# A fused tokenizer, phase-memory attention and top-2 mixture of experts on one core: less side work, a hand-written order, and two PSUM banks for the later pairs

## The chip, the cores and the metric

One core of a Trainium2 chip runs the whole kernel in one launch. The metric is the device time in microseconds (us) of one execution, as the median of several. The host only lays data out.

## The reference, cut to what matters

Sixteen images and sixteen texts become sixteen sequences of 272 tokens of 64 features; everything is fp32.

```python
h = tokenizer(x)                      # 2x2 conv, q, k, v, softmax over 144 tokens, output projection
h = concatenate([h, txt], axis=1)     # (16, 144 + 128, 64)
h = h + attention(layernorm(h))
h = h + experts(layernorm(h))

# attention: a content stream, a position stream, a mix of both
kp = tanh(tanh(x @ Wk1 + bk1) @ Wk2 + bk2) * pi      # 32 phases a token; qp the same with Wq
mem_re, mem_im = cumsum(cos(kp) * v_c), cumsum(sin(kp) * v_c)        # along the tokens
content = (mem_re * cos(qp) + mem_im * sin(qp)).sum() / sqrt(32 * pos)
position = (cumsum(v_p * cos_p) * cos_p + cumsum(v_p * sin_p) * sin_p) / sqrt(pos)
gate = softmax(relu(x @ Wg1 + bg1) @ Wg2 + bg2)
out = layernorm(gate[0] * position + gate[1] * content) @ Wo + bo    # with ln_g, ln_b

# experts: 8 of them, top 2 of a gate, computed for all tokens and weighted
for e in range(8):
    out += w[:, e] * (gelu(x @ W1[e] + b1[e]) @ W2[e] + b2[e])
```

## The kernel before, in words

Two sequences lie on the 128 partitions at once (64 features each), so there are 8 pairs of 272 columns, 2176 columns in all. For everything that works on tokens they are cut in 17 windows of 128 columns, in 5 groups of 3, 4, 4, 4 and 2 windows (`GW`). The stages are:

- Pairs, stage by stage: `qkv`, `scores`, `exps`, `probs_n`, `probs_t`, `mix`, `tok_out` (the tokenizer), then `hidden` and `phases` (tanh), `phase_abs`, `trig` (Sin), `content` and `content_b` (the content value and its bias), `values` and `streams` (the position value, and its cumulative sums), `memory` (key times query, masked: the cumulative sum written as a matrix) and `recall` (that matrix times the content value).
- Groups: `h0_t`, `ln1_stats`, `ln1_norm`, `xn_t`, `residual`, `mix_gate`, `gate_z`, `gate_t`, `gate_p` before the attention; `combine`, `ln2_stats`, `ln2_norm`, `norm_s`, `attn_out`, `ln3_stats`, `ln3_norm`, `xn2_t`, `route`, `route_t`, `weights_t`, `route_bias` behind it.
- Steps of the experts: `expert:i` (L1025; first product on TensorE, Gelu on ScalarE, L535) and `expert_out:i` (L1044; second product, times the routing weight on VectorE, L779, added up on GpSimd, L410), with i = 8 g + e for group g and expert e; `finish` transposes a group's sum and adds the residual.

One list, `PLAN` (L131), gives the order of all stages. Each engine walks through it and issues its own part, so every queue has this order and a waiting instruction holds up all behind it. `make_plan` (L114) makes the list from tables of slots and orders: a pair's or a group's stage stands at a fixed offset from the others. All of `recall:0` to `recall:7` stands ahead of `expert:1`. `WARM` puts `keep_warm` steps in the list: 22 matmuls on ones into bank 7 (L815) that compute nothing. SyncE has an order of its own (L336): routing rows out to DRAM and spread over the partitions into `wide` for group g + 1, then the store of group g.

PSUM has 8 banks. `hidden` writes 2 and 3, `phases` 4 and 5, `values` 0, `content` 1, `memory` 2 and 3 or 4 and 5 in turn, `recall` 1; `expert` 0 to 3, `expert_out` 4 or 5; the groups' stages use 6 and 7, for which `take` (L796) keeps the last reader and waits for it. So the first `expert` waits until all values, memories and recalls are read (L1028).

The layer norms are `moments` (L583: statistics block by block, then small operations) and `normalise` (L600): one VectorE operation for each block of 64 columns. Between them GpSimd takes the power -0.5 (L370). The bias of the experts is a product of its own for each group (`route_bias`: L1016 and a copy on VectorE, L771) with which the sum begins.

In `recall` the half h is the outer loop and the three chunks of tokens the inner one (L965); in `memory` the half is the inner one (L953). `phases` contracts over 128 rows of `attw`, half of which are zero (L937).

ScalarE functions by table: exps, then all tanh, then all Sin (`trig`, L502 and L504), then Gelu with the tanh of `route_t`.

Of the kernel before, what the change touches and what calls it, by code (L numbers as in the profile page):

```python
# [21 lines left out]
ACT = mybir.ActivationFunctionType  # L22
# [46 lines left out]
for _name, _n in [("kq1", 128), ("vc", 64), ("vp", 256), ("g1", 16), ("gate", 8)]:  # L69
# [8 lines left out]
PAIR_AT = {  # L78
    "qkv": (0, 0), "scores": (1, 1), "exps": (1, 4.7), "probs_n": (2, 0.5), "probs_t": (2, 4.5),
    "mix": (3, 3), "tok_out": (4, 4), "hidden": (9, 8), "phases": (10, 7.5), "phase_abs": (11, 0.4),  # L80
    "content": (11, 8.5), "content_b": (12, 0.5), "values": (15, 8.6), "streams": (16, 0.6),
    "memory": (18, 8), "recall": (20, 7.5),
}
LN1_AT = {
    "h0_t": (5, 2.5), "ln1_stats": (6, 0.2), "ln1_norm": (6, 8.7), "xn_t": (7, 2.7),
    "residual": (7, 6.5), "mix_gate": (8, 6.784), "gate_z": (9, 0.2), "gate_t": (9, 7.6),
    "gate_p": (10, 12.2),
}
FIRST_AT = {
    "combine": (-7, 7.682), "ln2_stats": (-7, 8.2), "ln2_norm": (-6, 9), "norm_s": (-4, 0.7),  # L90
    "attn_out": (-4, 8.41), "ln3_stats": (-4, 8.6), "ln3_norm": (-2, 0.7), "xn2_t": (-1, 0.7),
    "route": (-1, 4.204), "route_t": (0, 10.2), "weights_t": (1, 8.5), "route_bias": (1, 10.2),
}
LATER_AT = {
    "combine": (-10, 10.6), "ln2_stats": (-10, 12), "ln2_norm": (-8, 0.05), "norm_s": (-7, 5.5),
    "attn_out": (-7, 10.2), "ln3_stats": (-7, 12), "ln3_norm": (-6, 11.4), "xn2_t": (-4, 10.2),
    "route": (-4, 10.998), "route_t": (-2, 0.3), "weights_t": (-2, 10.1), "route_bias": (0, 10.3),
}
EXPERT_AT = {
    "expert": (0, 10), "expert_out": (1, 10.5),  # L100
}
TRIG_AT = [
    (18, 1), (18, 1.1), (19, 19.372), (19, 20), (20, 20), (21, 20), (22, 20.53), (23, 20),
]
EXPERTS = 28
LN1_SHIFT = [0, 0, 0, 0, 0]
SHIFT = [0, 1, 1, 1, 1]
WARM = [
    (10, 9.5, 2), (12, 9.5, 2), (13, 9.5, 2), (14, 9.5, 2), (15, 9.5, 2), (17, 9.5, 2), (27, 0.5, 4),
    (28, 10.05, 6),  # L110
]


def make_plan():  # L114

    plan = [(slot, order, "keep_warm", n) for slot, order, n in WARM]
    for b in range(NP):
        plan += [(slot + b, order, stage, b) for stage, (slot, order) in PAIR_AT.items()]
    plan += [(slot, order, "trig", b) for b, (slot, order) in enumerate(TRIG_AT)]
    for g in range(NG):  # L120
        plan += [(slot + LAST_PAIR[g] + LN1_SHIFT[g], order, stage, g) for stage, (slot, order) in LN1_AT.items()]
        start = EXPERTS + E * g
        steps = FIRST_AT if g == 0 else LATER_AT
        plan += [(slot + start + SHIFT[g], order, stage, g) for stage, (slot, order) in steps.items()]
        for e in range(E):
            plan += [(slot + start + e, order, stage, E * g + e) for stage, (slot, order) in EXPERT_AT.items()]
        plan.append((start + E + 1, 10.7, "finish", g))
    return [(stage, i) for _, _, stage, i in sorted(plan)]


PLAN = make_plan()  # L131


def fusion_block(nc, x_a, x_b, cols_d, tokw_d, phase_d, rows_d, attw_d, spl_d, txt_d, const_d, w1_d,
                 w2_d, b2_d, sel_d, out):
    with ExitStack() as ctx:
# [66 lines left out]
        vare = sb("vare", [128, 2, 8])  # L203
        rstd = sb("rstd", [128, 2, 8])
# [4 lines left out]
        ones = sb("ones", [128, L])  # L209
        cons = sb("cons", [128, COLS])  # L210
# [7 lines left out]
        c1 = sb("c1", [128, 512])  # L218
# [6 lines left out]
        k1 = sb("k1", [128, 8, 8])  # L225
        k2 = sb("k2", [128, 8, 8])
# [918 lines left out]
```

## Time and profile before

| | us |
|---|---|
| median of three runs | 320.4 |
| lowest and highest of them | 315.83, 320.89 |
| the profiled execution, its own time | 314.21 |
| its span, first to last instruction | 312.3 |
| busy: TensorE, VectorE, ScalarE, GpSimd | 277.1, 201.4, 152.2, 111.9 |
| weight loads, beside the matmuls | 145.7 |
| mean granted TensorE clock | 0.952 |

A row of the profile names a line of the kernel, an engine, what is written from what, how often, the busy time, the mean of one in ns, and the idle time before with what ended it. An fp32 matmul shows as two instructions. PE is TensorE, DVE VectorE, ACT ScalarE, POOL GpSimd, SPq the queue in which SyncE issues transfers.

### The profile page before, as it was taken

How to read it: one execution, taken by the hardware profiler on the slowest of the kernel's cores; microseconds unless marked ns; L12 is line 12 of the kernel's file. 1: busy time of each engine (PE TensorE's matmuls, PEld its weight loads, DVE VectorE, ACT ScalarE, POOL GpSimd, SP SyncE). 2: the span in 40 equal slices, each digit the busy share in tenths (PEclk: the TensorE clock that was granted, in tenths of full speed). 3: DMA queues.
4: the chain of work that ended last, by engine and by line, in shares of the span. 5: the costliest groups of instructions: out<-in, count | busy, mean ns of one | idle time of the engine just before them, and what ended most of it. 6: DMA issues, size and time to landing. Idle time of an engine off the chain costs nothing.

```text
span 312.3 us, 4746 instructions
## 1 busy us (share of the span) xinstructions
PE 277.1 (89%) x1576; PEld 145.7 (47%) x1576; DVE 201.4 (65%) x635; ACT 152.2 (49%) x299; POOL 111.9 (36%) x116
## 2 busy tenths in 40 slices
PE   8659795979788896999999889999899999999993
PEld 6547564556454553666445333333333333333551
DVE  4797877379458999858376674575745865645321
ACT  3768761455427531314545536544356546445461
POOL 1100235237627975310252242531524332432332
PEclk9999955699799998999999999999999999999998
DMA  7700000000000000000340291004710057000600
GB/s 244 258 7 1 2 0 0 0 2 1 0 2 2 2 0 0 3 0 0 79 127 0 66 210 25 2 0 104 168 35 3 0 121 173 14 0 4 168 4 17
DMA packets 12360, 14.42 MB, mean 46 GB/s; under 512 B 6097, under 2 KB 9985, under 8 KB 12209
## 3 DMA queue, kind: packets, MB, share of 16 engines
q1 hardware_dynamic: 11760, 13.66, 16.9%
q10 hardware_dynamic: 576, 0.47, 0.6%
q8 instruction: 13, 0.21, 0.3%
q14 instruction: 11, 0.08, 0.1%
HBM read 12.87 MB, written 1.25 MB: 45 GB/s over the span
## 4 chain that ended last, share of the span: by engine, by line
PE 61%; DVE 25%; issue 8%; POOL 2%; ACT 2%; DMA 1%; POOLq 0%; DVEq 0%
PE ps L1055 18%; PE ps L1041 16%; PE ps L968 4%; PE ps L815 3%; DVE arena L569 2%; PE ps L939 2%; PE ps L848 2%; DVE xn L603 2%; DVE early L685 2%; DVE early L680 2%; PE ps L994 2%; DVE early_p L638 1%; PE ps L884 1%; PE ps L1002 1%; DVE vs L779 1%
## 5 line engine op out<-in xcount | busy, mean ns | idle before, releaser
L535 ACT ACTIVATE arena<-ps,cols 128x1024 f32<-128x1024 f32 (+2 forms) x80 | 74.5, 982 | 61.0 <-PE ps L1041 60.9
L410 POOL TENSOR_TENSOR moe<-moe,vs 128x512 f32<-128x512 f32 (+2 forms) x40 | 44.3, 1107 | 91.2 <-DVE vs L779 91.0
L1041 PE MATMUL ps<-xt,w 64*128 64x512 f32 (+2 forms) x320 | 69.3, 551 | 0.0
L1055 PE MATMUL ps<-arena,w 128*64 128x512 f32 (+2 forms) x320 | 67.2, 541 | 0.0
L779 DVE TENSOR_TENSOR vs<-ps,wide 128x512 f32<-128x512 f32 (+2 forms) x40 | 24.4, 610 | 50.0 <-PE ps L1055 45.1
L370 POOL TENSOR_TENSOR rstd<-vare,minus_half 128x8 f32<-128x8 f32 (+2 forms) x15 | 22.8, 1521 | 65.0 <-DVE vare L597 65.0
L1041 PEld LDWEIGHTS ps<-xt,w 64*128 64x128 f32 x320 | 27.5, 186 | 33.5 <-issue 30.9
L1055 PEld LDWEIGHTS ps<-arena,w 128*64 128x64 f32 x320 | 19.4, 136 | 36.3 <-issue 30.5
L603 DVE TENSOR_SCALAR xn<-res,mean,rstd 128x64 f32<-128x64 f32 x68 | 20.0, 365 | 1.4 <-POOL rstd L370 1.4
L968 PE MATMUL ps<-early_p,vc 128*64 128x272 f32 (+2 forms) x96 | 18.9, 322 | 0.0
L968 PEld LDWEIGHTS ps<-early_p,vc 128*64 128x64 f32 (+1 forms) x96 | 11.0, 141 | 9.1 <-issue 6.1
L685 DVE TENSOR_TENSOR_SCAN early<-ones,early 128x272 f32<-128x272 f32 x16 | 14.4, 941 | 0.3
L603 DVE TENSOR_SCALAR comb<-comb,mean,rstd 128x64 f32<-128x64 f32 x34 | 11.6, 410 | 3.4 <-POOL rstd L370 3.4
L508 ACT ACTIVATE cons<-ps 128x272 f32<-128x272 f32 x8 | 3.2, 398 | 21.8 <-PE ps L968 21.8
L389 POOL TENSOR_TENSOR vc<-vc,rows 128x256 f32<-128x256 f32 x8 | 6.7, 832 | 17.1 <-ACT vc L493 17.1
L815 PE MATMUL ps<-ones 128*128 128x272 f32 x44 | 12.0, 407 | 0.6 <-DVE comb L716 0.6
L446 ACT ACTIVATE early_p<-ps,negmax 72x144 f32<-72x144 f32 x32 | 11.6, 372 | 0.4 <-DVE negmax L631 0.4
L848 PE MATMUL ps<-ident,early_p 72*72 72x72 f32 x64 | 6.5, 254 | 6.0 <-DVE early_p L638 6.0
L486 ACT ACTIVATE trig<-ps,cols 128x272 f32<-128x272 f32 x8 | 3.9, 487 | 16.1 <-PE ps L939 16.1
L691 DVE SCALAR_TENSOR_TENSOR trig<-trig,cols 128x544 f32<-128x544 f32 x8 | 6.3, 784 | 8.4 <-ACT trig L487 8.4
L588 DVE BATCH_NORM_STATS2 stat<-res 128x6 f32<-128x64 f32 x68 | 9.5, 210 | 3.1 <-ACT res L465 3.0
L939 PE MATMUL ps<-hid,attw 128*64 128x272 f32 x64 | 10.6, 459 | 0.0
(140 smaller groups left out, 440.6 us busy)
## 6 DMA issues: line engine op xcount, KB each, us to landing
wide<-rows_of SPq DMA_DIRECT2D x24, 256.0 KB, 5.7
wide<-rows_of SPq DMA_DIRECT2D x8, 192.0 KB, 4.0
w<-in_w SPq DMA_DIRECT2D x1, 1024.0 KB, 5.3
wide<-rows_of SPq DMA_DIRECT2D x8, 128.0 KB, 3.3
out<-res SPq DMA_DIRECT2D x6, 128.0 KB, 2.5
h0s<-in_txt SPq DMA_DIRECT2D x1, 512.0 KB, 6.8
w<-in_w SPq DMA_DIRECT2D x1, 512.0 KB, 6.1
arena<-in_x_a SPq DMA_DIRECT2D x1, 288.0 KB, 3.9
```

Of the source, the lines that this page charges most:

```text
L370: pool.tensor_tensor(rstd[:, g % 2, 0:nb(g)], vare[:, g % 2, 0:nb(g)], minus_half[:, 0:nb(g)], ALU.pow).then_inc(rstd_ok[kind], 1)
L410: pool.tensor_tensor(acc[:, g % 2, 0:128 * GW[g]], acc[:, g % 2, 0:128 * GW[g]], scaled[:, i % 2, 0:128 * GW[g]], ALU.add).then_inc(S["acc ...
L535: act.activation(hidden_e[:, k % 4, 0:2 * n].rearrange("p (h t) -> p h t", h=2), ps[:, 2 * j:2 * j + 2, 0:n], ACT.Gelu, bias=col("b1", 2 * ...
L603: ins = dve.tensor_scalar(dst[:, 64 * k:64 * k + 64], src[:, 64 * k:64 * k + 64], mean[:, g % 2, k:k + 1], rstd[:, g % 2, k:k + 1], ALU.su ...
L685: ins = dve.tensor_tensor_scan(cum[:, i % 2, k, :], ones[:, :], y[:, i % 2, k, :], 0.0, ALU.mult, ALU.add)
L779: dve.tensor_tensor(scaled[:, i % 2, 0:64 * n], ps[:, 4 + i % 2, 0:64 * n], wide[:, g % 2, i % E, 0:64 * n], ALU.mult).then_inc(S["scaled_ ...
L815: pe.matmul(ps[:, 7, 0:L], ones[:, 0:128], ones[:, :], start=True, stop=True)
L848: ins = pe.transpose(ps[0:SC, 2 + 2 * (i % 2) + h, SI * t + SC * c:SI * t + SC * c + SC], probs[0:SC, i % 2, 2 * h + c, SC * t:SC * t + SC ...
L939: ins = pe.matmul(ps[64 * h:64 * h + 64, 4 + r, 0:L], attw[:, 64 * r:64 * r + 64], hid[:, i % 2, h, :], start=True, stop=True)
L968: ins = pe.matmul(ps[64 * h:64 * h + 64, 1, m:L], vc[0:size, i, o:o + 64], mem[0:size, i % 2, h, MOFF[k]:MOFF[k] + L - m], start=(k == 0), ...
L1041: ins = pe.matmul(ps[:, 2 * j + h, 0:n], w1[r, c:c + 128], xt[r, GC[g]:GC[g] + n], start=True, stop=True)
L1055: ins = pe.matmul(ps[64 * h:64 * h + 64, 4 + i % 2, 0:n], w2[:, 2 * (i % E) + j, :], hidden_e[:, (2 * i + j) % 4, n * h:n * h + n], start= ...
```

## The change

- `PLAN` is now a list written out (`ORDER`). `keep_warm` and `route_bias` are gone; `values`, `memory`, `recall` and `streams` of the pairs 3 to 7 stand between the groups' stages and the steps `expert:0` to `expert:8`. `trig` no longer stands in one run: tanh, Sin and Gelu take turns.
- Banks: `memory` writes 2, 4, 2 for pairs 0 to 2 and then 6 and 7 for all; `values` 0 and from pair 3 on 6; `recall` 1 and from pair 3 on 7. All banks go through `take`.
- Layer norms: one subtraction of the mean over the whole group ahead of the wait for GpSimd, one multiplication behind it.
- `content_b` is gone: VectorE adds the bias as it reads PSUM, where ScalarE copied and GpSimd added. The two Sin of a pair are one; the two products and the two scans of `streams` are one each.
- The experts' bias is transposed once (`bias_t`) and added in the operation that applies the routing weight; the first expert of a group writes the sum itself, so that GpSimd adds 35 times, not 40.
- `recall` and `mix` change the order of their loops; `phases` contracts over 64 rows.

```diff
+MEM_BANK = [2, 4, 2, 6, 6, 6, 6, 6]
+VAL_BANK = [0, 0, 0, 6, 6, 6, 6, 6]
+REC_BANK = [1, 1, 1, 7, 7, 7, 7, 7]
...
+trig:0 trig:1 h0_t:4 phase_abs:2 content:3 trig:2 phases:3 ln1_norm:3 memory:0 gate_t:2 mix_gate:2 gate_z:2
+recall:0 ln1_stats:4 gate_p:1 memory:1 xn_t:3 hidden:4 streams:2 phase_abs:3 recall:1 memory:2 trig:3 combine:0
+phases:4 recall:2 ln2_stats:0 hidden:5 memory:3 ln2_norm:0 phase_abs:4 streams:3 ln1_norm:4 phases:5 values:3
+recall:3 phase_abs:5 norm_s:0 content:4 attn_out:0 mix_gate:3 xn_t:4 gate_z:3 ln3_stats:0 hidden:6 combine:1
+ln3_norm:0 trig:4 trig:5 content:5 gate_p:2 hidden:7 phases:6 memory:4 content:6 xn2_t:0 phases:7 ln2_stats:1
+memory:5 expert:0 ln2_norm:1 route:0 recall:4 phase_abs:6 gate_t:3 norm_s:1 route_t:0 expert:1 values:4 recall:5
+streams:4 content:7 weights_t:0 trig:6 attn_out:1 streams:5 gate_z:4 values:5 expert_out:0 expert:2 mix_gate:4
+expert_out:1 gate_t:4 ln3_stats:1 expert:3 memory:6 ln3_norm:1 expert:4 expert_out:2 phase_abs:7 expert_out:3
+xn2_t:1 gate_p:3 expert:5 route:1 expert_out:4 combine:2 expert:6 route_t:1 expert_out:5 expert:7 weights_t:1
+ln2_stats:2 trig:7 gate_p:4 expert_out:6 recall:6 values:6 streams:6 expert:8 memory:7 ln2_norm:2 expert_out:7
+recall:7 values:7 expert:9 streams:7 finish:0 residual:3 norm_s:2 expert_out:8 combine:3 expert:10 ln2_stats:3
...
+expert:22 weights_t:3 expert:23 expert_out:21 expert_out:22 expert:24 finish:1 expert:25 expert_out:23
+expert_out:24 expert:26 finish:2 route_t:4 expert:27 expert_out:25 expert_out:26 expert:28 weights_t:4
...
+                dve.tensor_tensor(blocks(dst[:, 0:n]), blocks(src[:, 0:n]), spread(mean[:, kind, g % 2, 0:nb(g)], nb(g)),
+                                  ALU.subtract).then_inc(centred[kind], 1)
+            def normalise(kind, g, dst):
+                n = nb(g)
                 dve.wait_ge(rstd_ok[kind], g + 1)
+                dve.wait_ge(centred[kind], g + 1)
+                return dve.tensor_tensor(blocks(dst[:, 0:64 * n]), blocks(dst[:, 0:64 * n]),
+                                         spread(rstd[:, kind, g % 2, 0:n], n), ALU.mult)
...
+                    act.activation(trig[:, :, L * i:L * i + L], trig[:, :, L * i:L * i + L], ACT.Sin,
                                    scale=col("sin_scale"), bias=col("sin_bias")).then_inc(S["trig_sb"], 1)
...
+                    dve.scalar_tensor_tensor(out=total, in0=ps[:, OUT_BANK[i % 2], 0:n], scalar=b2_col[:, e:e + 1],
+                                             in1=wide[:, g % 2, e, 0:n], op0=ALU.add, op1=ALU.mult)\
+                        .then_inc(S["scaled_sb"], 1)
...
+                    for h in range(2):
+                        for r in range(2):
+                            k = slice(64 * r, 64 * r + 64)
+                            ins = pe.matmul(ps[64 * h:64 * h + 64, 4 + r, 0:L], attw[k, 64 * r:64 * r + 64],
+                                            hid[k, i % 2, h, :], start=True, stop=True)
...
+                    for k, (m, size) in enumerate(MCH):
+                        for h in range(2):
                             o = 128 * k + 64 * h
+                            ins = pe.matmul(ps[64 * h:64 * h + 64, REC_BANK[i], m:L], vc[0:size, i, o:o + 64],
                                             mem[0:size, i % 2, h, MOFF[k]:MOFF[k] + L - m],
                                             start=(k == 0), stop=(k == len(MCH) - 1))
```

## Rows read from the trace of the kernel before

**Rows 1.** The page: engine TensorE, busy over the span, and the chain by line.

```profile
PE 277.1 (89%) x1576; PEld 145.7 (47%) x1576; DVE 201.4 (65%) x635; ACT 152.2 (49%) x299; POOL 111.9 (36%) x116
PE ps L1055 18%; PE ps L1041 16%; PE ps L968 4%; PE ps L815 3%; DVE arena L569 2%; PE ps L939 2%; PE ps L848 2%; DVE xn L603 2%; DVE early L685 2%; DVE early L680 2%; PE ps L994 2%; DVE early_p L638 1%; PE ps L884 1%; PE ps L1002 1%; DVE vs L779 1%
```

**Rows 2.** Busy by stretch: length, engines' busy (instructions), granted clock, DMA, GB/s.

```profile
0.00:9.00 9.00, 7.31 (x20) 5.39 (x20) 4.33 (x14) 4.27 (x6) 1.01 (x9) 1.00 0.74 224
9.00:34.50 25.50, 19.83 (x193) 15.78 (x193) 20.32 (x56) 19.04 (x72) 1.48 (x2) 1.00 0.22 77
34.50:58.00 23.50, 16.93 (x105) 11.79 (x104) 17.73 (x73) 10.82 (x40) 8.47 (x6) 0.62 0.00 1
58.00:98.00 40.00, 35.21 (x203) 21.28 (x204) 24.99 (x84) 18.05 (x49) 20.30 (x23) 0.92 0.00 1
98.00:143.00 45.00, 39.05 (x253) 25.25 (x252) 38.84 (x98) 15.60 (x33) 24.62 (x29) 0.96 0.00 1
143.00:306.00 163.00, 157.23 (x798) 65.52 (x798) 93.96 (x313) 84.37 (x103) 54.57 (x46) 1.00 0.26 62
```

**Rows 3.** The chain in order of time, TensorE's stages: start us, us on the chain.

```profile
93.31 1.07 PE ps L939 x8
...
126.20 1.05 PE ps L954 x12
127.73 2.12 PE ps L968 x12
...
157.93 1.49 PE ps L1041 x8
159.42 1.44 PE ps L1055 x8
```

**Rows 4.** Groups by line, TensorE and VectorE.

```profile
L815 PE MATMUL ps<-ones 128*128 128x272 f32 x44 | 12.0, 407 | 0.6 <-DVE comb L716 0.6
...
L1016 PE MATMUL ps<-wt,b 16*128 16x512 f32 (+2 forms) x10 | 5.0, 576 | 0.0
...
L603 DVE TENSOR_SCALAR xn<-res,mean,rstd 128x64 f32<-128x64 f32 x68 | 20.0, 365 | 1.4 <-POOL rstd L370 1.4
L603 DVE TENSOR_SCALAR comb<-comb,mean,rstd 128x64 f32<-128x64 f32 x34 | 11.6, 410 | 3.4 <-POOL rstd L370 3.4
L716 DVE TENSOR_TENSOR comb<-c 128x512 f32<-128x512 f32 (+2 forms) x5 | 4.1, 823 | 0.2
...
L712 DVE TENSOR_TENSOR c<-ps,p 128x512 f32<-128x512 f32 (+2 forms) x5 | 3.0, 605 | 1.0 <-PE ps L981 0.9
```

**Rows 5.** Timeline 70:75: GpSimd's and VectorE's operations beside each other.

```profile
70.14 1.27 POOL L384 TENSOR_TENSOR res<-res,xn 128x512 f32<-128x512 f32 x1
70.29 1.14 DVE L593 TENSOR_SCALAR mean<-msum 128x8 f32<-128x8 f32 x1
...
71.99 3.00 POOL L370 TENSOR_TENSOR rstd<-vare,minus_half 128x8 f32<-128x8 f32 x2 [0.58 <-DVE vare L597]
...
72.80 0.17 DVE L593 TENSOR_SCALAR mean<-msum 128x4 f32<-128x4 f32 x1
```

**Rows 6.** Timeline of ScalarE around the first Sin of the pairs.

```profile
99.27 1.28 ACT L502 ACT_TABLE_LOAD   x1
100.56 0.61 ACT L502 ACTIVATE trig<-trig,cols 128x272 f32<-128x272 f32 x1
```

**Rows 7.** Timeline of TensorE, `values` with the idle time ahead of it.

```profile
106.26 0.73 PE L917 MATMUL ps<-xt,vp_w 128*128 128x272 f32 x2 [0.73 <-DVE early L680]
...
121.81 0.95 PE L917 MATMUL ps<-xt,vp_w 128*128 128x272 f32 x2 [2.63 <-DVE early L680]
```

**Rows 8.** The transfers of the routing weights: SyncE's timeline, and the page's part 6.

```profile
250.96 0.33 SPq L326 DMA_DIRECT2D rows_of<-wt  x1
252.60 4.92 SPq L333 DMA_DIRECT2D wide<-rows_of  x8
...
wide<-rows_of SPq DMA_DIRECT2D x24, 256.0 KB, 5.7
```

More of the change, by code:

```diff
@@ L71 @@
 NSPL = sum(n for _, n in SPL.values())
[L78 to L128, printed above, removed]
@@ new lines @@
+probs_n:6 bias_t:0 values:0 gate_t:0 tok_out:4 ln1_norm:1 probs_t:5 probs_t:6 xn_t:1 scores:7 exps:7 mix_gate:1
+residual:1 mix:5 gate_z:1 hidden:0 gate_p:0 probs_n:7 streams:0 mix:6 tok_out:5 gate_t:1 probs_t:7 h0_t:2
+content:1 hidden:1 tok_out:6 ln1_stats:2 streams:1 values:1 phases:0 ln1_norm:2 mix:7 hidden:2 tok_out:7
+phases:1 h0_t:3 phase_abs:0 content:2 ln1_stats:3 xn_t:2 residual:2 phases:2 hidden:3 phase_abs:1 values:2
+trig:0 trig:1 h0_t:4 phase_abs:2 content:3 trig:2 phases:3 ln1_norm:3 memory:0 gate_t:2 mix_gate:2 gate_z:2
@@ new lines @@
+expert_out:9 expert:11 combine:4 ln2_norm:3 expert:12 ln2_stats:4 attn_out:2 ln2_norm:4 norm_s:3 expert_out:10
+ln3_stats:2 expert_out:11 expert:13 attn_out:3 norm_s:4 ln3_norm:2 expert_out:12 expert_out:13 expert:14
+ln3_stats:3 xn2_t:2 expert:15 route:2 route_t:2 attn_out:4 expert:16 residual:4 expert_out:14 ln3_stats:4
+expert_out:15 weights_t:2 ln3_norm:3 expert:17 expert_out:16 expert_out:17 expert:18 xn2_t:3 ln3_norm:4
+expert:19 xn2_t:4 route:3 expert:20 route_t:3 expert_out:18 expert_out:19 route:4 expert:21 expert_out:20
@@ L208, in fusion_block @@
         vc = sb("vc", [128, NP, 384])
-        ones = sb("ones", [128, L])
-        cons = sb("cons", [128, COLS])
+        cons = trig[:, 0, :]
+        ones = sb("ones", [128, 2 * L])
         gu = sb("gu", [128, 8, 16])
@@ L255, in fusion_block @@
         var_ok = [sem(f"var{k}") for k in range(3)]
+        centred = [sem(f"centred{k}") for k in range(3)]
         rstd_ok = [sem(f"rstd{k}") for k in range(3)]
@@ L646, in _ @@
                     dve.wait_ge(S["h0t"], i + 1)
-                    moments(0, i, res[:, cut(i)])
-                elif stage == "ln1_norm":
                     if i >= 2:
@@ L670, in _ @@
                         .then_inc(S["mg_p"], 1)
+                elif stage == "content":
+                    dve.wait_ge(S["vc_mm"], i + 1)
+                    if i == 0:
+                        dve.wait_ge(ld["rows"], 16)
+                    tail = MCH[2][1]
+                    dve.tensor_tensor(blocks(vc[:, i, 0:256]), blocks(ps[:, 1, 0:256]), over(row("bvc"), 4), ALU.add)
+                    dve.tensor_tensor(blocks(vc[0:tail, i, 256:384]), blocks(ps[0:tail, 1, 256:384]),
+                                      row("bvc")[0:tail, :].unsqueeze(1).to_broadcast([tail, 2, 64]), ALU.add)\
+                        .then_inc(S["vc_sb"], 1)
                 elif stage == "streams":
@@ L806, in _ @@
             for _ in range(WARM_UP):
-                pe.matmul(ps[:, 7, 0:L], ones[:, 0:128], ones[:, :], start=True, stop=True)
+                pe.matmul(ps[:, 7, 0:L], ones[:, 0:128], ones[:, 0:L], start=True, stop=True)
             for stage, i in PLAN:
@@ L814, in _ @@
                     for _ in range(i):
[L815 removed]
+                        pe.matmul(ps[:, 7, 0:L], ones[:, 0:128], ones[:, 0:L], start=True, stop=True)
                 elif stage == "qkv":
@@ L856, in _ @@
                     take(7, "mix_sb", i + 1)
-                    for h in range(2):
-                        for t in range(2):
+                    for t in range(2):
+                        for h in range(2):
                             k = 2 * t + h
```

287 lines of the change are left out of this document (121 added, 166 removed).

## The prediction, made blind

> **What bounds the kernel now.** I read the page first. TensorE is busy 277.1 of 312.3 us, VectorE 201.4, ScalarE and GpSimd half or less; on the chain TensorE's lines lead, the two expert products with 34% [rows 1]. An average hides the stages, so I cut the span where stages change [rows 2]. From 143 to 306 us, the experts, TensorE works 157.2 of 163.0 us (96.5%): it is the bound and nothing else is near. Before 143 us it works 7.3 + 19.8 + 16.9 + 35.2 + 39.1 = 118.3 us (82.7%), and 9.0 of these are keep_warm (12.0 us in 44 instructions, 12 of which come after 143) [rows 2, 4]. VectorE works 4.3 + 20.3 + 17.7 + 25.0 + 38.8 = 106.2 us there (74.3%), and 38.8 of 45 us from 98 to 143, where TensorE waits for it ahead of `values`, 0.73 us once and 2.63 us once [rows 2, 7]. The clock stands at 0.62 of full from 34.5 to 58 us, that is mostly at 1.2 GHz and not 2.4, and close to full elsewhere. So there are two machines: a front of 143 us in which engines wait for each other, and a back of 163 us that is pure TensorE. The question is how much of the back can be put in the holes of the front, and what TensorE has less to do.
>
> **TensorE, removed and shortened.** keep_warm: 12.0 us. route_bias: 5.0 us busy, 4.7 by start to start. `recall` takes 2.12 us, `memory` 1.05 with the same column counts (272, 144, 16), the same twelve instructions, and the half as the inner loop, so that two neighbours use different halves of the array [rows 3]. The new loop of `recall` is of that kind: 8 x (2.12 - 1.05) = 8.6 us. `mix` I cost at nothing; it has no row of either kind for comparison and is short (bounds: 0 and 1 us). `phases` is now four products in four quarters of the array. It takes 1.07 us [rows 3]; if still only two run together nothing is gained, if four, half: 0 to 4.3 us over eight pairs. No row has four; I take the middle, 2.1. `bias_t` adds 0.2.
>
> **VectorE.** Norms cost 20.0 + 11.6 = 31.6 us now [rows 4]. After, 30 operations over whole groups, six passes over the five groups. A pass costs 4.1 us by the addition of two SBUF tiles, 3.0 by the product that reads PSUM [rows 4]: 24.6 or 18.0 us, a gain of 7.0 to 13.6; I take 10, two thirds of it in the front. The bias copy goes (3.0, as the L712 row), the content bias comes: 8 x 0.59 = 4.7 (256 and 128 columns, by the L712 row scaled), and two start-ups a pair are saved, -1. The bias inside `expert_out` costs nothing: the same operands pass once. In all VectorE falls from 201 to 192 us.
>
> One thing in the norms speaks against the change. While GpSimd adds two tiles (1.27 us), a VectorE operation on eight columns took 1.14 us instead of 0.17 [rows 5]; while GpSimd takes its powers the same operation took 0.17. The new subtraction stands just beside the power, so it is not held; it would be held by an expert's addition, at most 35 x 1.1 us. The Trainium skill, SBUF — State Buffer, section SBUF: two separate sides, says that a VectorE operation with two SBUF inputs and a GpSimd operation that reads SBUF lock each other out for the whole instruction; by that rule each of the 15 powers would hold the subtraction for its length, 22 us of VectorE, and push the time towards rival 1. The trace agrees for the addition and disagrees for the power.
>
> **ScalarE.** It loses the content copies (about 5 us) and half of the Sin start-ups. But functions take turns now: along the new order I count Sin runs at trig:0-2, 3, 4-5, 6 and 7, each with a load before and after, instead of one: 8 or 9 more loads at 1.28 us [rows 6], 10.3 to 11.5 us. ScalarE is busy 68 of 143 us in the front, so the engine has room; what waits behind a load is `phases` or a Gelu, and TensorE has other steps queued. I take 0 on the path, 11.5 as the other end. In the trace the Sin starts right at the end of the load, at 100.56, so a switch is 1.28 us [rows 6]. The Trainium skill, ScalarE: Activation LUTs, section What ACT_TABLE_LOAD costs, gives about 2.66 us a switch with its drain, which would make 24 us, an estimate; no drain shows in this trace behind the load.
>
> **SyncE.** The weight transfer of group 3 stands behind the store of group 1, whose `finish:1` has moved to behind `expert:24`. From there: rows out and back 1.6 us, landing 5.7, with issue some 8 us [rows 8]. Behind the waiting `expert_out:24` on VectorE queue all later ones and TensorE needs bank 4 again at `expert_out:26`; between lie three `expert`, three `expert_out` and a `finish` of TensorE, 3 x 1.92 + 3 x 1.87 + 0.5 = 11.9 us (four windows each, the rows of three windows scaled by columns gives as much within 0.1 [rows 3]). Hidden, with 4 us to spare; if the cover fails it costs up to 8.
>
> **The move, and the sum.** I compare at the last `recall`. Ahead of it now stand nine `expert` (8 x 1.49 and one of four windows, 1.9), eight `expert_out` (8 x 1.44) and transposes and products of groups 0 and 1 (6.4 us by the same kind of row): 31.6 us of TensorE moved from back to front [rows 3]. Front, TensorE: 118.3 - 9.0 - 8.6 - 2.1 + 0.2 + 31.6 - 0.6 (`values:7` goes back) = 129.8 us. Back: 157.2 - 31.6 - 4.7 - 3.0 + 0.6 = 118.5 us, at today's 96.5% 122.8 us, and the last 6.3 us (312.3 - 306) stay. VectorE's front: 106.2 + 24.5 - 6.7 + 4.7 - 1 = 127.7 us; the 24.5 moved are two `combine` (4.1), three sets of statistics (6.3) and three norms (5.6, old price), `attn_out` 0.7, `route` and two `route_t` 5.8, eight weighted products at 0.53 (4.3), less `streams:7` (2.3), lengths read off VectorE's timeline.
>
> How dense is the new front? Today 82.7% for TensorE. For it: free steps of experts now lie between the dependent ones, norms have a shorter end (one multiplication instead of eight operations behind the power). Against it: keep_warm, which filled waits, is gone; and VectorE would have to stand at 81% (127.7 of 157), above its 74% today, though it reaches 86% from 98 to 143. I take today's density: 129.8 / 0.827 = 157.0. Span: 157.0 + 122.8 + 6.3 = 286.1, with the 1.9 us around it 288.0 for an execution like the profiled one. That one took 314.2 where the three runs had a median 6.2 above and a lowest 1.6 above; I add 3 and forecast 291 us.
>
> **Rivals.**
> 1. VectorE binds the front: its share stays at 74.3%. 127.7 / 0.743 = 171.9; 171.9 + 122.8 + 6.3 + 1.9 + 3 = 306. For: rows 7, waits for VectorE today; against: 86% in 98 to 143.
> 2. The interleaving does all it can: the front reaches 92%, close to the back. 129.8 / 0.92 = 141.1; 275 us. For: the back shows 96.5% with the same cross-engine steps; against: the first 60 us have no expert to put in.
> 3. The loads of tables are exposed, each with its 1.28 us, and so are the 8 us of the weight transfer: 291 + 11.5 + 8 = 310.
> 4. Slower: banks 6 and 7. From `memory:3` to `recall:7` 29 stages take one of the two, 16 of them, by the lengths used here, with under 1.5 us of TensorE between the last writer and the next. Each may wait for the reader as `values` does today: 0.73 and 2.63, mean 1.7 us [rows 7]. 29 x 1.7 = 49 us, less 9.5 us of idle time that 82.7% already grants to this stretch (46 us of TensorE): 291 + 40 = 331. It decides from (320.4 - 291 + 9.5) / 29 = 1.3 us a stage on. Against: most stages have an expert step between, and `memory`'s reader needs one us.
> 5. The clock falls further without keep_warm. Today it is at half from 34.5 to 58 us at 16.9 us of work; another 20 us at half add up to 8 us: inside the range, no case of its own.
>
> **How the numbers follow.** Forecast 0.5; rival 1: 0.15; rival 2: 0.18; rival 3: 0.1; rival 4: 0.05; 0.02 for what I don't see. 2% either way is about what a measurement of this kernel can tell. Under 314 us: forecast, 1, 2 and 3 nearly all, 0.9; within 2%: 0.06; slower 0.04. The range goes from 274 (rival 2 with `phases` at its best) to 309 (rival 1, and 3 in part).
>
> **What would show it.** `recall` at about 1.05 us; `phases` at 0.55 or 1.07; 13 or 14 table loads; VectorE near 192 us busy, norms near 22; TensorE near 250 us busy; the last `recall` near 157 us, and 129 us from there to the end. Wrong would be: a last `recall` behind 170 us with waits for VectorE (rival 1), waits of TensorE for readers of banks 6 and 7 of over 1 us each (rival 4), idle time of TensorE behind ScalarE's loads (rival 3), or a back that is no longer over 95% dense.

## The result, and the profile after

The changed kernel takes 263.55 us (median of four, 261.54 to 265.10), the kernel before 318.12 in the same series (315.36 to 320.89): 0.835 times, 95% interval 0.825 to 0.845. In some executions of most kernels here, in half of those of the kernel before, the granted clock is lower and the time over 1.5% longer, and the ratios and the times compared from here on leave these out, which gives 315.6 us before, 263.55 after and a gain of 52 us. The forecast was 291, the range ended at 274. The direction was right and the gain was nearly twice the forecast's. The profiled execution took 261.54 us, its span is 259.6, its mean granted clock 0.986.

The page of the changed kernel, busy by engine and the chain by line, answers to [rows 1]:

```profile
PE 239.1 (92%) x1523; PEld 126.2 (49%) x1523; DVE 176.9 (68%) x558; ACT 155.8 (60%) x286; POOL 98.4 (38%) x87
...
PE ps L996 25%; PE ps L1009 24%; PE ps L929 2%; DVE stat L557 2%; DVE arena L538 2%; PE ps L918 2%; PE ps L942 2%; DVE negmax L602 2%; PE ps L963 2%; DVE trig L671 2%; DMA phase<-in_phase 1%; PE ps L955 1%; PE ps L811 1%; PE ps L858 1%; DVE early_p L682 1%
```

TensorE's share rose from 89 to 92% although it works 38 us less, and the two expert products (L996, L1009) hold half of the chain where they held a third.

Busy by stretch, with the columns of [rows 2]. The first expert starts at 95.55 us (before: 143.9), the last `recall` ends at 136.4 (before: 143.0):

```profile
0.00:9.00 9.00, 7.48 (x20) 5.50 (x20) 4.17 (x13) 4.11 (x6) 1.33 (x10) 1.00 0.77 224
9.00:40.00 31.00, 24.77 (x232) 19.55 (x233) 27.23 (x95) 23.36 (x92) 6.86 (x5) 1.00 0.18 64
40.00:60.00 20.00, 18.78 (x162) 12.04 (x161) 18.34 (x60) 14.63 (x40) 9.48 (x7) 1.00 0.00 1
60.00:95.50 35.50, 28.85 (x236) 19.29 (x236) 33.08 (x105) 22.19 (x38) 14.24 (x10) 0.90 0.01 1
95.50:136.30 40.80, 40.29 (x273) 21.69 (x271) 35.38 (x110) 27.56 (x37) 18.72 (x15) 1.00 0.28 67
136.30:254.80 118.50, 118.50 (x607) 47.97 (x603) 57.63 (x178) 63.91 (x77) 47.00 (x40) 1.00 0.26 61
254.80:259.60 4.80, 0.43 (x3) 0.20 (x2) 1.11 (x2) 0.00 (x0) 0.72 (x1) 0.98 0.39 82
```

There are three machines now. Up to 40 us little has changed. From 40 to 95.5 us VectorE works 18.34 + 33.08 = 51.4 of 55.5 us (93%); from 50 to 85 us the chain of waits is its own with few breaks, so it sets the pace there. Up to 60 us TensorE is as full (18.78 of 20 us). Before, VectorE was as dense over a shorter stretch, and fuller:

```profile
100.00:120.00 20.00, 16.48 (x118) 10.38 (x116) 19.80 (x36) 9.47 (x20) 16.01 (x19) 1.00 0.00 1
```

From 95.5 us on TensorE works 40.29 of 40.8 us and then 118.50 of 118.50, while at first four recalls, three values, two memories and 17 expert steps share its queue.

The products whose order or shape changed, on TensorE's timeline (start, us, how many), beside [rows 3]:

```profile
53.53 0.69 PE L907 MATMUL ps<-hid,attw 64*64 64x272 f32 x8
...
98.36 1.14 PE L929 MATMUL ps<-early_p,vc 128*64 128x272 f32 x12
99.43 0.66 PE L948 MATMUL ps<-ident,comb 128*128 128x128 f32 x4
```

`recall` (L929) takes 98.36 to 99.43, start to start: 1.07 us where it took 2.12. `phases` (L907) takes 0.62 us on the chain of waits (at 90.26), where it took 1.07.

The norms on VectorE and the other groups that changed, beside [rows 4]:

```profile
L576 DVE TENSOR_TENSOR xn<-xn,rstd 128x512 f32<-128x512 f32 (+2 forms) x10 | 7.6, 763 | 0.5 <-POOL rstd L356 0.5
...
L569 DVE TENSOR_TENSOR xn<-res,mean 128x512 f32<-128x512 f32 (+2 forms) x10 | 6.0, 604 | 0.0
...
L576 DVE TENSOR_TENSOR comb<-comb,rstd 128x512 f32<-128x512 f32 (+2 forms) x5 | 3.4, 679 | 1.0 <-POOL rstd L356 1.0
...
L569 DVE TENSOR_TENSOR comb<-comb,mean 128x512 f32<-128x512 f32 (+2 forms) x5 | 3.0, 604 | 0.0
```

Together 20.0 us where the block-by-block operations took 31.6.

ScalarE's table loads, groups by line:

```profile
L468 ACT ACT_TABLE_LOAD x5 | 6.4, 1283 | 0.1
...
L504 ACT ACT_TABLE_LOAD x3 | 3.8, 1283 | 0.3 <-PE ps L1009 0.2
...
L462 ACT ACT_TABLE_LOAD x2 | 2.6, 1283 | 0.0
```

With one each at L401, L407, L422 and L458 there are 14, where there were 5. Nine stand ahead of the first expert, where there were four.

### The profile page after: what moved, and what is told of

It reads as the page before. It is cut to its first block, busy times and chain, and to the rows that moved or that the text cites. A ratio compares the mean times of both kernels' runs of the same rounds, so it can differ in the third digit from the quotient of the medians.

```text
span 259.6 us, 4570 instructions
## 1 busy us (share of the span) xinstructions
PE 239.1 (92%) x1523; PEld 126.2 (49%) x1523; DVE 176.9 (68%) x558; ACT 155.8 (60%) x286; POOL 98.4 (38%) x87
## 3 DMA queue, kind: packets, MB, share of 16 engines
q1 hardware_dynamic: 11760, 13.66, 20.7%
## 4 chain that ended last, share of the span: by engine, by line
PE 70%; DVE 20%; issue 5%; DMA 1%; POOL 1%; ACT 1%; POOLq 0%; DVEq 0%
PE ps L996 25%; PE ps L1009 24%; PE ps L929 2%; DVE stat L557 2%; DVE arena L538 2%; PE ps L918 2%; PE ps L942 2%; DVE negmax L602 2%; PE ps L963 2%; DVE trig L671 2%; DMA phase<-in_phase 1%; PE ps L955 1%; PE ps L811 1%; PE ps L858 1%; DVE early_p L682 1%
## 5 line engine op out<-in xcount | busy, mean ns | idle before, releaser
L996 PE MATMUL ps<-xt,w 64*128 64x512 f32 (+2 forms) x320 | 69.8, 554 | 0.0
L386 POOL TENSOR_TENSOR acc<-acc,vs 128x512 f32<-128x512 f32 (+2 forms) x35 | 39.5, 1129 | 70.8 <-DVE vs L759 70.6
L1009 PE MATMUL ps<-arena,w 128*64 128x512 f32 (+2 forms) x320 | 65.2, 538 | 0.0
L759 DVE SCALAR_TENSOR_TENSOR vs<-ps,b_col,wide 128x512 f32<-128x512 f32 (+2 forms) x35 | 23.3, 667 | 35.7 <-PE ps L1009 32.7
L996 PEld LDWEIGHTS ps<-xt,w 64*128 64x128 f32 x320 | 27.3, 185 | 32.0 <-issue 23.9
L1009 PEld LDWEIGHTS ps<-arena,w 128*64 128x64 f32 x320 | 20.2, 136 | 36.5 <-issue 34.3
L374 POOL TENSOR_TENSOR early<-early,turn_n 128x544 f32<-128x544 f32 x8 | 11.6, 1456 | 22.6 <-DVE early L665 22.6
L422 ACT ACTIVATE early_p<-ps,negmax 72x144 f32<-72x144 f32 x32 | 11.6, 373 | 2.3 <-DVE negmax L602 2.2
L665 DVE TENSOR_TENSOR_SCAN early<-ones,early 128x544 f32<-128x544 f32 x8 | 11.3, 1411 | 0.3
L759 DVE SCALAR_TENSOR_TENSOR acc<-ps,b_col,wide 128x512 f32<-128x512 f32 (+2 forms) x5 | 3.3, 670 | 11.8 <-DMA wide<-rows_of 4.5
L929 PE MATMUL ps<-early_p,vc 128*64 128x272 f32 (+2 forms) x96 | 9.9, 325 | 1.4 <-DVE early_p L684 1.3
L448 ACT ACTIVATE xt<-ps 128x256 f32<-128x256 f32 (+1 forms) x18 | 5.9, 373 | 7.9 <-PE ps L858 7.9
L918 PE MATMUL ps<-trig 64*128 64x272 f32 (+2 forms) x96 | 9.4, 312 | 0.9 <-ACT trig L468 0.8
L918 PEld LDWEIGHTS ps<-trig 64*128 64x128 f32 (+1 forms) x96 | 7.3, 165 | 5.0 <-ACT trig L468 1.9
L929 PEld LDWEIGHTS ps<-early_p,vc 128*64 128x64 f32 (+1 forms) x96 | 6.0, 143 | 7.4 <-issue 3.3
L682 DVE TENSOR_TENSOR early_p<-ps,mask 128x832 f32<-128x832 f32 x8 | 8.1, 1014 | 0.9 <-PE ps L918 0.9
L576 DVE TENSOR_TENSOR xn<-xn,rstd 128x512 f32<-128x512 f32 (+2 forms) x10 | 7.6, 763 | 0.5 <-POOL rstd L356 0.5
## 6 DMA issues: line engine op xcount, KB each, us to landing
arena<-in_x_a SPq DMA_DIRECT2D x1, 288.0 KB, 4.1
```

The lines of the kernel that those rows point to most:

```text
L374: link(pool.tensor_tensor(cum[:, i % 2, :, :], cum[:, i % 2, :, :], turn_n[:, :, :], ALU.mult))
L386: pool.tensor_tensor(acc[:, g % 2, 0:128 * GW[g]], acc[:, g % 2, 0:128 * GW[g]], scaled[:, i % 2, 0:128 * GW[g]], ALU.add).then_inc(S["acc ...
L422: ins = act.activation(probs[0:SC, i % 2, k, :], ps[0:SC, 2 + 2 * (i % 2) + k // 2, SI * (k % 2):SI * (k % 2) + SI], ACT.Exp, bias=negmax[ ...
L759: dve.scalar_tensor_tensor(out=total, in0=ps[:, OUT_BANK[i % 2], 0:n], scalar=b2_col[:, e:e + 1], in1=wide[:, g % 2, e, 0:n], op0=ALU.add, ...
L918: ins = pe.matmul(ps[0:size, MEM_BANK[i] + h, MOFF[k]:MOFF[k] + L - m], trig[r, 0, L * i + m:L * i + m + size], trig[r, 1, L * i + m:L * i ...
L929: ins = pe.matmul(ps[64 * h:64 * h + 64, REC_BANK[i], m:L], vc[0:size, i, o:o + 64], mem[0:size, i % 2, h, MOFF[k]:MOFF[k] + L - m], start ...
```

## The experiments

Each version ran four times (`joined_sin` six, `before_loops` ten), beside the kernel before on the same chip, whose median lies between 314.9 and 317.5 us by chip. Every time is a median of three to nine executions; for `late_experts` and `old_banks` it is a single one, with the range of the others in brackets and no ratio. "The changed kernel" is 263.55 us. Four questions: order or work, what of the order, what of the work, and the clock.

### Order or work

`old_order` has all of the changed kernel's work in the order and banks of before, keep_warm included. `old_work` is the new order and banks with the old norms, loops, content copies, Sins, products and scans (the experts' bias stays new, keep_warm stays out).

```diff
-ORDER = """ ... """
+PLAN = make_plan()                # tables and WARM of before; bias_t added
+MEM_BANK = [2, 4, 2, 4, 2, 4, 2, 4]; VAL_BANK = [0] * 8; REC_BANK = [1] * 8
```

> The changed kernel's work in the order and the banks of the kernel before, keep_warm steps included (the content bias stands on VectorE where GpSimd had it). If the order carries the gain (theory 1): about 295 to 303 us; only TensorE's shorter recall and phases where they are on the path (5 us), route_bias (5 us) and VectorE's shorter norms (5 to 10 us) are won against 318. If it is the lighter side work (theory 2): 275 us or less, most of the 55 us.

> The new order and banks with the side work of before: norms block by block, content bias on ScalarE and GpSimd, two Sin, two products and two scans a pair, old loops of recall, phases and mix (the experts' bias stays new). If the parts add up, 263.5 + 14.3 (norms) + 4.7 (loops) + 3 to 6 for the rest: 286 to 289 us. If the order alone is worth what it was in the other comparison (306.5 - 263.5 = 43): before less 43 = 277. If the new order needs the light side work, the parts more than add up: over 295.

Measured: `old_order` 306.5 us against 315.7 before, 0.972 [0.961, 0.982]; `old_work` 282.3 against 317.5, 0.887 [0.875, 0.899].

| | old order | new order |
|---|---|---|
| old work | 315.7 to 317.5 | 282.3 |
| new work | 306.5 | 263.6 |

The order is worth 35 us with the old work and 43 with the new, the lighter work 9 us in the old order and 19 in the new. Neither does it alone, and they help each other by 8 to 10 us. One piece of work sits in the wrong place: the experts' bias is new in `old_work` too, so its 5.0 us of TensorE [rows 4] count as order there. Without them, an estimate, the order is worth 30 us with the old work, and the two help each other by some 13. `old_order` came out above what theory 1 had (295 to 303), `old_work` between two of its cases.

### What of the order: interleaving

`late_experts` moves the nine `expert` and eight `expert_out` steps that stand ahead of the last `recall` behind it, nothing else. `late_warm` is the same with 32 keep_warm products put in ten of the places.

```diff
-... xn2_t:0 ... memory:5 expert:0 ln2_norm:1 ... route_t:0 expert:1 values:4 recall:5 ... recall:7 values:7 expert:9
+... xn2_t:0 ... memory:5 ln2_norm:1 ... route_t:0 values:4 recall:5 ... recall:7 expert:0 expert:1 ... values:7 expert:9
```

> The changed kernel's order, with its nine expert and eight expert_out steps that stand ahead of the last recall moved behind it in their own order; all else as changed. Interleaving with experts is what fills (theory 1a): from 95 us on VectorE has about 31 us of other work to the last recall and TensorE 15, so that stretch shrinks only from 41 to 33 us while the back grows by 25: 280 to 283 us. If the order of the rest of the front carries the gain (theory 1b): under 270 us.

> The late experts (295.3) with 32 keep_warm matmuls in ten places in the stretch that the experts left, on ones and into bank 7. If the interleaved experts paid as heat, by keeping the clock at 2.4 GHz: the clock of that stretch rises from 0.6 to 0.9 and the time falls to 285 or less. If they paid as work done in the holes: within 4 us of 295.

Measured: `late_experts` 290.5 us (295.1 to 295.9; the profiled one is at 295.1), `late_warm` 296.2, 0.942 [0.936, 0.947]. Of the order's 43 us the interleaving carries 27, 32 by the bracketed ones; the rest of the order 11 to 16. Both cases of the expectation had `late_experts` lower, at 283 us or less.

Busy by stretch of `late_experts`, columns as above:

```profile
0.00:95.50 95.50, 78.92 (x623) 55.99 (x624) 80.01 (x253) 62.52 (x167) 31.91 (x32) 0.93 0.13 43
95.50:120.00 24.50, 15.82 (x99) 10.15 (x98) 19.84 (x70) 8.03 (x16) 6.78 (x6) 0.75 0.21 51
120.00:150.00 30.00, 20.76 (x96) 11.88 (x98) 15.42 (x51) 9.90 (x14) 5.54 (x4) 0.58 0.36 84
150.00:290.00 140.00, 138.41 (x709) 55.58 (x709) 62.71 (x186) 75.20 (x90) 53.40 (x46) 1.00 0.18 44
```

and its longest waits of TensorE (line, released by, us in total, times, longest):

```profile
PE ps L970 <- DVE wsp L739: 3.6, 1, 3.6
PE ps L858 <- DVE xn L576: 3.6, 1, 3.6
PE ps L918 <- issue: 3.0, 1, 3.0
```

Its last `recall` starts at 140.2 us without one expert ahead; the changed kernel's starts at 135.2 with seventeen steps ahead. The moved steps cost the front nothing. What they fill are waits of 1 to 3.6 us, for the routing weights (L739), for a norm (L576), ahead of a `memory` (L918; the trace names no releaser): chains that run through several engines.

The clock had been the other explanation: without experts it stands at 0.75 and 0.58 in these stretches. `late_warm` tells them apart. Its windows:

```profile
95.50:120.00 24.50, 14.93 (x102) 10.74 (x101) 18.45 (x58) 6.21 (x11) 8.21 (x6) 0.92 0.28 66
120.00:150.00 30.00, 24.26 (x133) 15.97 (x133) 13.62 (x48) 8.92 (x13) 4.10 (x3) 0.95 0.32 72
```

The clock is at 0.92 and 0.95, the last `recall` starts at 142.6 us, no earlier than 140.2, and the time didn't fall. The test isn't quite clean: the filler products wait themselves for the readers of bank 7 (9.1 us in sum, mostly for the VectorE lines for which useful products waited before), so a small gain of the clock could hide in it. 27 us could not: useful work in the holes pays, warmth alone doesn't.

### What of the order: banks 6 and 7

```diff
-MEM_BANK = [2, 4, 2, 6, 6, 6, 6, 6]; VAL_BANK = [0, 0, 0, 6, 6, 6, 6, 6]; REC_BANK = [1, 1, 1, 7, 7, 7, 7, 7]
+MEM_BANK = [2, 4, 2, 4, 2, 4, 2, 4]; VAL_BANK = [0] * 8; REC_BANK = [1] * 8
```

> The changed kernel with the later pairs' values in bank 0, memories in 2 to 5 and recalls in 1, as before, in the new order. Each of these now waits for a Gelu or a weighted product of the expert before and holds up the next expert: 13 such stages from the first expert on at 1 to 2 us: 8 to 20 us slower (theory: the banks are needed). If VectorE binds there anyway: within 3 us.

Measured: 271.6 us (277.4 to 280.6), so the two banks are worth some 8 us, 14 to 17 by the bracketed ones. In the profiled run, the fastest, the last `recall` starts at 144.4 us and not 135.2, and the first expert at 99.0 and not 95.6: most of the loss falls where experts and pairs share banks 0 to 5. It went the other way round than rival 4 had it: the apartness is a gain.

### What of the work

`old_norms` (the changed kernel with the norms block by block), the same in the old order (`old_order_norms`), `old_loops` (the changed kernel with the old `recall`, `phases` and `mix`), and `before_loops` (the kernel before with the new ones).

```diff
 # old_norms, old_order_norms
-                dve.tensor_tensor(... src, mean, ALU.subtract)          # whole group, ahead of the wait
-                dve.wait_ge(rstd_ok[kind], g + 1)
-                return dve.tensor_tensor(... dst, rstd, ALU.mult)
+                dve.wait_ge(rstd_ok[kind], g + 1)
+                for k in range(nb(g)):
+                    ins = dve.tensor_scalar(dst[...], src[...], mean[...], rstd[...], ALU.subtract, ALU.mult)
 # before_loops (old_loops is the reverse)
-                    for h in range(2):
-                        for k, (m, size) in enumerate(MCH):
+                    for k, (m, size) in enumerate(MCH):
+                        for h in range(2):
```

> The changed kernel with the layer norms of before: one VectorE operation for each 64 columns behind GpSimd's power. VectorE then has about 10 us more, and each of the seven norms ahead of the first expert ends 1.2 us later. Theory 1 (the front is a chain through VectorE): 5 to 10 us slower, 268 to 273. Theory 2 (TensorE binds, norms are hidden behind expert steps): under 3 us.

> The changed kernel's work in the old order, and the norms of before besides; to be held against the run of the old order (306.5). Theory 1 (a short norm pays where the order is dense): 2 to 6 us slower, 308 to 313, against 14.3 us in the new order. If a norm is worth the same in either order: 320, and the gains of order and work add up.

> The changed kernel with the loops of recall, phases and mix of before. TensorE has 8 x (1.07 + 0.46) = 12.2 us more. If TensorE bound all of it, 275 us; if VectorE binds the front, where all but recall 4 to 7 and two phases stand, about 4 to 6 us, 268 us.

> The kernel before with the new loops of recall, phases and mix alone. TensorE has 12.2 us less, all of it in the front. VectorE and waits bind there (theory 1): 2 to 6 us faster than before, as with its undoing in the new order (4.6). If TensorE's work counted in full: 12 us.

Measured: `old_norms` 277.8 us, 0.878 [0.868, 0.888]; `old_order_norms` 310.6, 0.986 [0.977, 0.996]; `old_loops` 268.2, 0.851 [0.843, 0.859]; `before_loops` 313.8 against 316.1, 0.995 [0.989, 1.000]. The norms are worth 14.3 us in the new order, more than the 5 to 10 expected, and 4 in the old (310.6 - 306.5, of two chips; their intervals overlap). The loops are worth 4.6 us in the new order and some 2 in the old, where the interval touches no gain. Norms and loops add up to the 19 us of the lighter work in the new order, so the merged Sins, products and scans and the content bias are worth nothing that these runs can tell; none of them was undone by itself.

The norms' groups in `old_norms`, and its longest waits of TensorE:

```profile
L572 DVE TENSOR_SCALAR xn<-res,mean,rstd 128x64 f32<-128x64 f32 x68 | 23.8, 419 | 1.9 <-POOL rstd L356 1.9
...
L572 DVE TENSOR_SCALAR comb<-comb,mean,rstd 128x64 f32<-128x64 f32 x34 | 8.6, 324 | 1.7 <-POOL rstd L356 1.7
```

```profile
PE ps L856 <- DVE xn L572: 3.9, 4, 2.0
PE ps L927 <- DVE early_p L682: 3.1, 1, 3.1
```

VectorE has 23.8 + 8.6 - 20.0 = 12.4 us more to do in the norms. The first expert starts at 109.5 us, 14 us later than in the changed kernel, and from there on the two run nearly alike (the last `recall` starts 40.7 us behind the first expert here, 39.7 there). So the loss arises ahead of the experts. VectorE's added work doesn't explain it: up to the first expert it works 88.4 us here and 82.8 there, 5.5 us more for 14 us of time, and from 40 to 109.5 us it is busy 84%, not 93%. What else is longer is each norm's end behind the power (up to eight operations and not one), and the clock is lower: 0.74 from 40 to 60 us and 0.86 from there to 109.5, where the changed kernel has 1.00 and 0.90. No run tells these two apart. In the old order the norms' groups of `old_order` sum to 24.2 us, those of `old_order_norms` to 32.8: 8.6 us of VectorE for 4 of time.

### Table loads

`more_loads` puts a one-column Exp into a spare tile behind the Sin of each pair, `loads_early` behind those of pairs 0, 1 and 4, `loads_late` of 6 and 7; `joined_sin` moves phase_abs:7 and trig:7 to behind those of pair 6. By their profiles these have 22, 20, 16 and 12 loads, the changed kernel 14.

```diff
                    act.activation(trig[...], trig[...], ACT.Sin, ...)
+                    if i in (0, 1, 4):
+                        act.activation(spare[:, i:i + 1], col("half_pi"), ACT.Exp)
```

> The changed kernel with a one-column Exp behind each pair's Sin, which brings some eight more loads of tables at 1.28 us (13 to about 21). Hidden, as ScalarE has room: under 3 us slower. On the path: 10 us slower, and then the loads of the change itself cost about as much.

> The changed kernel with a one-column Exp behind the Sin of pairs 0, 1 and 4: six more loads of tables, all ahead of the first expert. The nine added in the other run cost 9.5 us. If loads cost where the front is a chain: 7 to 9 us slower than 263.5.

> The changed kernel with a one-column Exp behind the Sin of pairs 6 and 7: two more loads, among the expert steps, where TensorE is over 98% busy. If loads are hidden there: within 1 us of 263.5. If each costs its length: 2.6 us slower.

> The changed kernel with phase_abs:7 behind phase_abs:6 and trig:7 behind trig:6, so that two loads of tables fall away. If a load costs what nine added ones did on average (9.5 us / 9): 2.1 us faster, 261.4. If only loads ahead of the first expert cost: same within 1 us, for here the back is dense.

Measured: `more_loads` 273.0 us, 0.861 [0.856, 0.866]; `loads_early` 271.7, 0.862 [0.857, 0.867]; `loads_late` 265.6, 0.842 [0.837, 0.848]; `joined_sin` 263.6, 0.837 [0.832, 0.843]. Eight loads more cost 9.4 us, six early ones 8.1 (1.35 each, the load with the small Exp), two late ones 2.0, which is within the spread, and two late ones fewer give nothing. (The expectations that speak of nine added loads mean these eight.) Ahead of the experts loads are on the path; among them they are all or nearly hidden. Two waits of TensorE in `more_loads` show where some are exposed; at the same two stages it waits 0.7 and 0.4 us in the changed kernel:

```profile
PE ps L870 <- ACT res L442: 4.4, 1, 4.4
PE ps L909 <- ACT trig L464: 2.4, 1, 2.4
```

### The clock

`before_warm` adds eight keep_warm products to the kernel before where the clock is at half; `old_order_cold` is `old_order` with none.

```diff
 WARM = [
-    (10, 9.5, 2),
+    (8, 3.5, 2), (8, 8.5, 2), (9, 4.5, 2), (9, 8.5, 2), (10, 9.5, 2),
```

> The kernel before with eight more keep_warm matmuls in four places from some 40 to 58 us, where the granted clock was at half. If that stretch at half speed holds the front up: the clock there rises over 0.9 and the time falls by 3 to 8 us (matmuls alone took 8 us longer). If the front there waits for VectorE and ScalarE anyway: no change within 2 us.

> As old_order, without the 22 keep_warm matmuls. If they only fill waits (theory 1): within 3 us of old_order. If the clock needs them in this order: the granted clock falls below 0.95 and the time is 5 to 15 us above old_order. If they themselves held work up: 5 to 8 us below old_order, which is their share of the chain before.

Measured: `before_warm` 317.8 us against 316.1, 1.012 [1.001, 1.022]; `old_order_cold` 308.7, 0.977 [0.963, 0.992], 2 us above `old_order`, which the intervals don't tell apart. The third to fifth stretch of [rows 2], in `before_warm`:

```profile
34.50:58.00 23.50, 17.39 (x125) 11.70 (x123) 17.70 (x73) 11.14 (x40) 9.42 (x7) 0.92 0.01 1
58.00:98.00 40.00, 35.21 (x210) 21.52 (x206) 27.29 (x87) 19.31 (x51) 20.81 (x25) 0.96 0.00 1
98.00:143.00 45.00, 39.04 (x230) 24.92 (x230) 35.01 (x84) 13.58 (x29) 23.19 (x27) 0.85 0.00 1
```

The clock from 34.5 to 58 us went from 0.62 to 0.92, and the first `phases` started 1.2 us earlier (57.4 and not 58.6), the first `recall` 2.1 us (104.8 and not 106.9). So TensorE at half clock had mostly, but not only, stretched its work into time that it would have waited: its products alone had taken some 7 us longer. The kernel as a whole gained nothing, for the clock fell elsewhere: from 120 to 130 us it is 0.50 in this run and 0.83 before, two `recall` take 3.9 us each, and the first expert starts at 146.1 us and not 143.9. The time of the run is therefore no clean price of the stretch at 0.62.

## Why the prediction was wrong in size

For an execution like the profiled one the forecast was 288.0 us; it took 261.5. Of the 26.5 us between them, 20.7 lie ahead of the last `recall` (157.0 forecast, 136.3 measured), 4.3 behind it, 1.5 in the last transfers.

**The step that failed** is "How dense is the new front?", with its answer "I take today's density: 129.8 / 0.827". TensorE's work there is 7.48 + 24.77 + 18.78 + 28.85 + 40.29 = 120.2 us, and 120.2 / 136.3 = 88.2%. At today's 82.7% this work would have given 145.3 us; so 11.7 of the 20.7 us are work that I had too much of (9.6 us at that density), and 9.0 are density.

- **The work, -9.6 us.** 7.0 us of it are durations at half clock. Seven groups with unchanged work (`mix_gate`, `probs_t`, `mix`, `tok_out`, the norms' transposes, `hidden`, the content product) sum to 44.1 us before and 37.1 after; `mix` for one took 1.23 us three times in the stretch at 0.62 and 0.72 elsewhere. I carried the stretched durations into the new front. The old density was inflated by the same time: at full clock it would have been some (118.3 - 7.0) / 143 = 78%, an estimate, and like for like the density rose by ten points, not by five. The 9.0 us of keep_warm were inflation too: I took them out of the work and left them in the 82.7%. Without them the estimate for useful work is 72%. `phases` gave 1.5 us more than taken.
- **The density.** Rival 2, the interleaving, was the right mechanism; TensorE works 99% from 95.5 us on, where the experts stand, though 88% over the front. Its 275 us are the nearest of all cases and still 11 too many. I gave it 0.18. `late_experts` shows it as the largest single part of the change, 27 to 32 us. I had costed the moved 31.6 us at their own work over the density, so at 38 us of front. The expert steps are 25.3 of them, at 31 us of front, and `late_experts` shows that they cost the front nothing. That is the general fault: steps that only fill holes were divided by a density as if they made holes of their own.
- **The back, -4.3 us.** Its work was forecast at 118.5 us and is 118.5. I left it today's 3.5% of idle time; there is none. Of its 5.8 us TensorE waited 3.0 for the routing weights (L1009, for VectorE's L761) and 2.2 in `finish` for the copy of the bias (L1022, for L771). The copy is gone, and no such wait is left at the weights.
- **Rival 1, VectorE.** The right engine, for another stretch. In the whole front it works 118.2 of 136.3 us, 87% and not 74%; it sets the pace only between 40 and 95.5 us, at 93%. A share of the past was no ceiling, and the past had shown it: 19.80 of 20 us from 100 to 120.
- **Table loads, "0 on the path".** Wrong for the early ones. Five more than before stand ahead of the first expert; at the 1.35 us of `loads_early` that would be some 7 us, an estimate, covered by the larger errors on the other side. For the four more among the experts it was right (`joined_sin`, `loads_late`).
- **Rival 4, banks.** Wrong in sign: the old banks cost 8 us or more. Behind the first expert TensorE waits for hardly anything (40.29 of 40.8 us busy); the order puts an expert step between most writers and readers, as I had written down as "against".
- **The weight transfer of group 3** is hidden for TensorE, as forecast: VectorE's first product of a group (L759) waits 4.5 us for transfers in sum, and TensorE none, behind 136.3 us.

**What came as forecast.** `recall` 1.07 us (forecast 1.05), `mix` no gain, `phases` between the bounds at the four-quarter end, 14 loads (13 or 14), norms 20.0 us of VectorE (21.6 as taken), the work of the back to a tenth. VectorE in all is 176.9 us, forecast 192: the norms are 1.6 us of that, the scans 2 (11.3 us where 14.4 stood, 1 us taken), and 6.6 are three small operations with the same work: one on `k` (L756, now L734) takes 215 ns in the mean and not 978, one each on `gu` and `zg` 272 and 271 and not 564 and 565. Against it, the bias in `expert_out`, taken at nothing, costs some 2 us (667 ns in the mean where 610 stood).

**GpSimd beside VectorE.** I had set the subtraction right beside the power and costed it as not held, and it takes 604 ns, as the product that reads PSUM in [rows 4] (605). This doesn't test the rule of the Trainium skill, SBUF — State Buffer, section SBUF: two separate sides, by which the one of the two that starts first has the ports for its whole length and the other waits: the subtraction starts 0.17 us ahead. What is longer is the power on eight columns, 2.02 us here and in `old_order` and `old_banks`, and 1.65 before, in `before_loops` and in `old_order_norms`, which lack the subtraction; that agrees with the rule. What disagrees is that a power, once it runs, doesn't hold VectorE for its whole length: an operation with two SBUF inputs takes its usual 0.78 us inside a power, here a row of GpSimd's timeline and one of the chain.

```profile
60.03 2.02 POOL L356 TENSOR_TENSOR rstd<-vare,minus_half 128x8 f32<-128x8 f32 x1 [2.05 <-DVE vare L566]
...
61.16 0.78 DVE trig L671
```

For GpSimd's products and additions the rule goes on agreeing. Timeline of VectorE:

```profile
79.14 0.78 DVE L671 SCALAR_TENSOR_TENSOR trig<-trig,cols 128x544 f32<-128x544 f32 x1
...
82.17 1.86 DVE L671 SCALAR_TENSOR_TENSOR trig<-trig,cols 128x544 f32<-128x544 f32 x1
```

and of GpSimd in the same microseconds:

```profile
82.02 1.43 POOL L374 TENSOR_TENSOR early<-early,turn_n 128x544 f32<-128x544 f32 x1 [3.39 <-DVE early L665]
```

The same operation took 0.78 us alone and 1.86 beside GpSimd's product, 1.1 us more. The row of GpSimd starts 0.15 us ahead and lasts 1.43.

**Of the table loads** the runs say 1.2 to 1.35 us each where nothing hides them, which is the row's 1.28 and no more. The Trainium skill, ScalarE: Activation LUTs, section What ACT_TABLE_LOAD costs, has about 2.66 us with the drain; by that the eight of `more_loads` would cost 21 us, an estimate, and they cost 9.4. These runs don't agree with it, and no drain shows in the trace: ScalarE's idle time ahead of the five loads at L468 is 0.1 us in sum.

## What to carry to other kernels

Split a span at the seams and ask of each stretch which work waits on chains and which is ready at any time; ready work that was moved into a stretch full of short waits cost nothing there (25.3 us of expert steps), so don't divide such work by the old density. Before a busy share is carried over, bring it to full clock and take filler products out: both count as busy and neither is work. The same edit is worth more in one schedule than in another (the norms 14.3 us in the new order, 4 in the old), so weigh the edits in the new schedule and not in the old. And a share over a long front hides short stretches in which an engine is full.

## What was not expected of the hardware

- A stretch of TensorE at 0.62 of the clock cost little: 1.2 to 2.1 us of what follows, for some 7 us of longer products; and with the experts removed the profiled execution took 296.2 us at a mean clock of 0.976 and 295.1 at 0.911. Filler products in one stretch didn't keep the clock up in a later one (0.50 from 120 to 130 us in `before_warm`).
- A subtraction on VectorE beside GpSimd's power lengthened the power, from 1.65 to 2.02 us on eight columns, and wasn't longer itself.
- Four fp32 products on four 64 x 64 quarters of the array took little more than half the time of two halves: eight instructions of 272 columns in 0.62 us, 1.07 on two halves. `mix` ran as fast with the half outside (0.72 us, `old_loops`) as inside (0.71), where `recall` took twice as long with it outside; no run tells why.
- Still open: which wait a single early table load lengthens; how the loss of `old_norms` divides between the norms' longer end and the clock; why the last `recall` starts later with less to do (4.9 us in `late_experts`, 7.3 in `late_warm` at nearly full clock); and how much of the 11 to 16 us of the order beside the interleaving are the banks. No version among the runs beat the changed kernel; `joined_sin` equals it.
